# Four-layer transformer on one core: the order of the overlapped pieces of layers three and four rewritten on all five engines

## The chip, the core and the metric

The kernel runs on one NeuronCore of a Trainium2 chip. Its engines are TensorE (PE: matrix products; PEld is its weight load), VectorE (DVE), ScalarE (ACT), GpSimd (POOL) and SyncE (SP, which here only issues DMAs); each runs its own instruction list in order, and they meet by semaphores. The metric is the device time of one execution in microseconds (us).

## The reference

x has 8 sequences (batches) of 512 tokens by 128. Four layers follow one another, each `x = x + attn(layernorm(x)); x = x + ffn(layernorm(x))`. All attentions have 16 heads of 8.

```
layer 1: causal attention without softmax;  ffn = 8 gated experts, two used
layer 2: linear attention with elu+1;       ffn = top-1 of 8 experts (relu), with a capacity
layer 3: softmax attention, |q-k| <= 32;    ffn = silu(x Wg) * (x Wu) Wd, hidden 384
layer 4: rope; k and v from a 64-wide latent; softmax over pages of 32 tokens,
         page(k) <= page(q);                ffn = top-1 of 8 experts (exact gelu, hidden 512)
```

The program counts the layers from 0, so that `l2_` and `l3_` name pieces of layers three and four.

## The kernel before

The program stands in stages with a barrier between them. The table `ORDER2` sets the stage of layers three and four (in the trace from about 481 to 1140 us). For each engine it is a list of pieces; the n-th occurrence of a name is that piece of batch n (0 to 7), here written with the batch behind a dot, `l2_q.4`. A piece is a handful of instructions. The lists are all that decides an engine's order: `for name, b in ORDER2["PE"]` and the like walk through them, and every engine waits by semaphores for what a piece needs. The lists lay layer three of batch b+1 over layer four of batch b. No planner runs inside the kernel; the lists are written out.

The pieces, by what TensorE does in them and the line of its matmuls:

- `l2a_n`, `l2f_n`, `l3a_n`, `l3f_n`: transposes of normalised rows (L611). Ahead of them DVE takes statistics (`..._s`), POOL the power -1/2, DVE normalises; ACT copies the transposes out of PSUM.
- `l2_q` (L899, L900), `l2_v` (L907), `l3_q`, `l3_lat`, `l3_k` (L999), `l3_v` (L1008): projections. `l3_k` comes from the latent that `l3_lat` makes.
- `l2_m0..3` (L917 mask, L925 scores) and `l3_m0..21` (L1022): scores of which DVE takes row maxima (L1701, two reductions a piece; L1710, one a piece). `l2_n1`/`l3_n1` (POOL) and `l2_n2`/`l3_n2` (L672) bring the maxima as extra rows into the stacked Q and K.
- `l2_e0..3` (L939, L948) and `l3_e0..9` (L1039): scores again, less the maximum, transposed; ACT takes exp (L1981, L1993). `l2_o0..3` (L962) and `l3_b0..9` (L1055): products with V. `l3_b` writes to a PSUM bank of its own and takes no buffer of the ring named below.
- `l2_t`, `l2_u`, `l2_j` (L645, L654, L663), and the same for `l3`: transposes, division, output projection; DVE adds it to x (L1162). `l2f_0..2` and `l2f_o` (L976, L977, L985): the feed-forward part of layer three. `l3t_r` (L626), `l3t_c`: router of layer four.

The queries and keys are split into three bf16 parts (`l2_p1`, `l2_p2`, `l3_p1`, `l3_p2` on ACT and POOL) and spread over partitions by 12 DMAs a batch and layer, which SP issues one after the other (L2233), from `l2_p2` or `l3_p2` in its list. `l3_m0` of a batch waits for all 12 of its batch. For batch 0 ACT issues five of them.

PSUM has a ring of three buffers for this stage. Each piece takes one (`l2_m`, `l2_e`, `l3_e`: two) in the order of TensorE's list, and a buffer is free when its reader has drained it. So a piece waits too for the reader of the piece three buffers back.

Of the kernel before, what the change touches and what calls it, by code (L numbers as in the profile page):

```python
# [149 lines left out]
for n in range(4, len(PLAN3)):  # L150
# [40 lines left out]
        l2a_n l2_q l2_v l2_m0 l2_m1 l2a_n l2_m2 l2_m3 l2_n2 l2_q l2_e0 l2_e1 l2_o0 l2_e2 l2_o1 l2_e3 l2_o2 l2_o3 l2_t l2_u l2_j l2_v l2a_n l2f_n  # L191
        l2f_0 l2f_1 l2f_2 l2_q l2f_o l2_m0 l3a_n l3_q l3_lat l3_k l3_v l2_m1 l2_m2 l2_m3 l2_n2 l3_m0 l3_m1 l2_e0 l3_m2 l2_e1 l3_m3 l3_m4 l2_o0 l2_e2
        l3_m5 l3_m6 l2_o1 l2_e3 l3_m7 l2_o2 l3_m8 l3_m9 l3_m10 l2_o3 l2_t l3_m11 l3_m12 l2_u l3_m13 l3_m14 l2_j l3_m15 l3_m16 l3_m17 l2_v l3_m18
        l2f_n l3_m19 l3_m20 l2f_0 l2f_1 l3_m21 l2f_2 l3_n2 l2f_o l3_e0 l2_m0 l3_e1 l3_b0 l2_m1 l3a_n l3_b1 l3_e2 l3_q l3_lat l3_e3 l3_k l3_b2 l3_v
        l2_m2 l3_e4 l3_b3 l2_m3 l3_e5 l3_b4 l3_e6 l3_b5 l2_n2 l2a_n l3_e7 l3_b6 l3_m0 l3_e8 l3_m1 l2_e0 l3_m2 l2_e1 l3_m3 l3_m4 l2_o0 l3_m5 l2_q
        l3_m6 l3_m7 l2_o1 l3_m8 l2_e2 l3_m9 l2_e3 l3_m10 l2_o2 l3_m11 l3_m12 l2_o3 l3_m13 l2_t l3_m14 l3_b7 l2_u l3_m15 l3_m16 l2_j l3_e9 l3_m17
        l3_m18 l3_b8 l2_v l3_b9 l3_m19 l2f_n l3_m20 l3_m21 l2f_0 l2f_1 l2f_2 l3_n2 l3_t l2f_o l3_e0 l3_u l2_m0 l3_e1 l3_b0 l3_j l3a_n l3_e2 l3_lat
        l3_q l2_m1 l3_b1 l3_k l3_e3 l3_b2 l2_m2 l3_e4 l3_b3 l2_m3 l2a_n l3_v l3_e5 l3_b4 l2_n2 l3f_n l3_e6 l3_b5 l3t_r l3_e7 l3_m0 l2_e0 l3_m1 l2_q
        l3_m2 l3_m3 l2_o0 l2_e1 l3_b6 l3_m4 l3_e8 l2_o1 l3_m5 l2_e2 l3_m6 l2_e3 l3_m7 l3_m8 l2_o2 l3_m9 l3_m10 l3_m11 l2_o3 l2_t l3_b7 l3_m12 l2_u
        l3_m13 l3_m14 l2_j l3_e9 l3_m15 l3_m16 l3_b8 l2_v l3_m17 l2f_n l3_m18 l3_m19 l3_m20 l2f_0 l3_m21 l2f_1 l2f_2 l3_b9 l3_t l3_n2 l2f_o l3_u  # L200
        l3_e0 l2_m0 l3_e1 l3_b0 l3t_c l3_j l3a_n l2_m1 l3_lat l3_q l3_e2 l3_b1 l3_k l3_e3 l3_b2 l3_v l2_m2 l3_e4 l3_b3 l2_m3 l3_e5 l3_b4 l3f_n l3_e6
        l3_b5 l2a_n l3t_r l2_n2 l3_e7 l3_m0 l2_q l3_m1 l2_e0 l3_m2 l3_m3 l3_b6 l2_e1 l3_m4 l2_o0 l3_m5 l2_e2 l3_m6 l3_m7 l2_o1 l3_m8 l2_e3 l3_m9
        l3_m10 l2_o2 l3_e8 l3_m11 l3_m12 l2_o3 l3_m13 l2_t l3_m14 l3_b7 l2_u l3_m15 l2_j l3_e9 l3_m16 l3_m17 l3_b8 l2_v l3_m18 l2f_n l3_m19 l3_m20
        l2f_0 l3_m21 l2f_1 l2f_2 l3_b9 l3_n2 l3_t l3t_c l2f_o l3_e0 l3_u l2_m0 l3_b0 l3_e1 l3_j l3a_n l3_e2 l3_q l3_lat l3_b1 l3_k l3_e3 l3_b2 l2_m1
        l3_e4 l3_b3 l3f_n l2_m2 l2_m3 l3_b4 l3_e5 l3t_r l3_v l2a_n l2_n2 l3_e6 l3_m0 l3_b5 l3_e7 l2_q l3_m1 l2_e0 l3_m2 l2_e1 l3_m3 l3_m4 l2_o0 l2_e2
        l3_m5 l3_m6 l2_o1 l3_m7 l3_m8 l2_o2 l3_m9 l2_e3 l3_m10 l3_m11 l3_b6 l3_m12 l2_o3 l3_m13 l2_t l3_e8 l3_m14 l2_u l3_m15 l3_m16 l2_j l2_v l3_m17
        l3_b7 l3_m18 l3_b8 l3_e9 l3_m19 l2f_n l3_m20 l3_m21 l2f_0 l2f_1 l2f_2 l3_n2 l3_b9 l3_t l3t_c l2f_o l3_e0 l3_u l2_m0 l3_e1 l3_b0 l2_m1 l3_j
        l3a_n l3_e2 l3_q l3_lat l3_b1 l3_e3 l3_k l3_b2 l3_v l2_m2 l3_e4 l3_b3 l2a_n l2_m3 l3_e5 l3_b4 l3f_n l3_e6 l3_b5 l2_n2 l3t_r l3_e7 l2_q l3_m0
        l2_e0 l3_m1 l2_e1 l3_m2 l3_b6 l3_m3 l3_e8 l2_o0 l3_m4 l2_e2 l3_m5 l3_m6 l2_o1 l2_e3 l3_m7 l3_m8 l2_o2 l3_m9 l3_m10 l3_m11 l2_o3 l2_t l3_m12
        l3_m13 l2_u l3_m14 l3_b7 l3_m15 l2_j l3_m16 l3_e9 l3_b8 l3_m17 l3_m18 l2_v l3_b9 l3_m19 l2f_n l3_m20 l3_m21 l2f_0 l2f_1 l2f_2 l3_n2 l3_t  # L210
        l2f_o l3_e0 l3_u l2_m0 l3_e1 l3_b0 l3t_c l3_j l3a_n l2_m1 l3_q l3_lat l3_e2 l3_k l3_b1 l3_e3 l3_b2 l2_m2 l3f_n l2_m3 l3t_r l3_e4 l3_b3 l3_e5
        l3_b4 l3_e6 l2_n2 l3_b5 l3_e7 l3_m0 l3_m1 l3_b6 l3_m2 l2_e0 l3_m3 l2_e1 l3_m4 l3_m5 l2_o0 l3_m6 l2_e2 l3_m7 l3_m8 l2_o1 l3_m9 l3_e8 l3_m10
        l2_e3 l3_m11 l3_m12 l2_o2 l3_m13 l3_m14 l2_o3 l2_t l3_v l3_m15 l2_u l3_m16 l3_m17 l2_j l3_b7 l3_e9 l3_m18 l3_m19 l3_b8 l3_b9 l2f_n l3_m20
        l3_m21 l2f_0 l2f_1 l2f_2 l3_t l3_n2 l2f_o l3_u l3t_c l3_e0 l3_e1 l3_b0 l3a_n l3_j l3_q l3_lat l3_k l3_e2 l3_b1 l3f_n l3_e3 l3_b2 l3t_r l3_e4
        l3_b3 l3_e5 l3_b4 l3_e6 l3_b5 l3_m0 l3_m1 l3_m2 l3_m3 l3_b6 l3_v l3_m4 l3_m5 l3_e7 l3_m6 l3_m7 l3_m8 l3_m9 l3_m10 l3_b7 l3_m11 l3_e8 l3_m12
        l3_e9 l3_m13 l3_m14 l3_m15 l3_m16 l3_b8 l3_m17 l3_m18 l3_m19 l3_b9 l3_m20 l3_m21 l3_n2 l3t_c l3_t l3_e0 l3_u l3_e1 l3_b0 l3_j l3_e2 l3_b1
        l3_e3 l3_b2 l3_e4 l3_b3 l3_e5 l3_b4 l3f_n l3_e6 l3_b5 l3t_r l3_e7 l3_b6 l3_e8 l3_b7 l3_e9 l3_b8 l3t_c l3_b9 l3_t l3_u l3_j l3f_n l3t_r l3t_c
    """,
# [2275 lines left out]
```

## Time and profile before

| what | us |
|---|---|
| runs | 1254.84, 1254.14, 1248.28; median 1254.14 |
| the profiled execution, its own time | 1255.06 |
| its span | 1253.3 |
| the stage of layers three and four in it | about 481 to 1140 |
| TensorE busy in the span | 1050.0 |

The span is from the first to the last instruction in the trace; 1.8 us of the profiled execution lie around it. In the view of stretches, each row gives the length of a stretch, what each engine was busy in it, and the clock that TensorE was granted as a share of 2.4 GHz. In the view in order of time, a row is a start, a duration, and in brackets the idle time before it with what ended that.

### The profile page before, as it was taken

Reading aid. Unit: us, or ns where it says so; the run is one execution under the profiler, and the core shown is the slowest. Engines: PE = TensorE matmul, PEld = TensorE weight load, DVE = VectorE, ACT = ScalarE, POOL = GpSimd, SP = SyncE. Lnnn points to the kernel's source line nnn. Section 1 sums busy time; section 2 is a strip of 40 time slices with the busy share of each in tenths; the row PEclk is TensorE's granted clock in tenths of the full one; section 3 lists DMA queues with packets and bytes.
Section 4 is the critical chain, followed back from the end, with each engine's and each line's share of the span. In section 5 each row is a group of like instructions: output and inputs, shape, how many; then the busy total and the mean of one; then the engine's idle time right before and its main releaser. Section 6 shows DMA issues by size and latency. Waiting matters only on the chain.

```text
span 1253.3 us, 38908 instructions
## 1 busy us (share of the span) xinstructions
PE 1050.0 (84%) x16739; PEld 769.8 (61%) x16739; DVE 821.0 (66%) x2329; ACT 553.8 (44%) x993; POOL 448.6 (36%) x538
## 2 busy tenths in 40 slices
PE   6889859999976996776888889888888887987984
PEld 4767637888864573544556656556665555463884
DVE  6889865679965113466769587786958685735332
ACT  4233202476642331333374656556484655261441
POOL 2134341336755244033122315042332404022675
PEclk9899979999976999999999999999999999998998
DMA  9464515643240413114022222112222202002884
GB/s 366 191 236 193 212 41 186 215 157 98 66 163 32 140 52 88 30 53 103 16 64 65 55 54 62 44 48 57 68 60 65 63 3 72 10 23 83 204 191 93
DMA packets 83725, 126.02 MB, mean 101 GB/s; under 512 B 13025, under 2 KB 64610, under 8 KB 83138
## 3 DMA queue, kind: packets, MB, share of 16 engines
q1 hardware_dynamic: 66863, 106.47, 26.5%
q0 software_dynamic: 10928, 13.64, 4.5%
q10 hardware_dynamic: 5763, 3.43, 1.1%
q8 instruction: 131, 2.15, 0.7%
q14 instruction: 40, 0.33, 0.1%
HBM read 50.82 MB, written 46.74 MB: 78 GB/s over the span
## 4 chain that ended last, share of the span: by engine, by line
PE 40%; DVE 26%; POOL 8%; issue 8%; ACT 7%; DMA 7%; SPq 3%; PEldq 1%; ACTq 0%; DVEq 0%; POOLq 0%; PEld 0%
DVE mx L1710 7%; POOL xs L2131 3%; PE ps L1022 2%; SPq L2233 2%; ACT MW L1993 2%; PE ps L787 2%; PE ps L774 2%; PE ps L775 2%; DMA K<-spm 2%; PE ps L962 2%; PE ps L880 2%; PE ps L865 2%; PE ps L976 2%; DVE bst L1134 2%; PE ps L1055 2%
## 5 line engine op out<-in xcount | busy, mean ns | idle before, releaser
L1710 DVE TENSOR_REDUCE mx<-ps 128x2 f32<-128x1024 f32 (+3 forms) x176 | 191.0, 1122 | 52.2 <-PE ps L1022 51.8
L1993 ACT ACTIVATE MW<-ps 128x1024 f32<-128x1024 f32 x160 | 154.6, 1030 | 81.2 <-PE ps L1039 80.9
L2131 POOL DMA_INDIRECT xs<-xr,sidu x96 | 96.7, 1007 | 122.2 <-DVE sidu L1293 87.5
L2074 POOL TENSOR_SCALAR rst<-bmv 128x4 f32<-128x4 f32 x64 | 16.5, 258 | 339.3 <-DVE bmv L1137 338.6
L1055 PE MATMUL ps<-MW,Vp 128*18 128x128 f32 x2560 | 87.4, 278 | 4.4 <-ACT MW L1993 2.3
L1022 PE MATMUL ps<-K,Q 64*128 64x512 bf16 (+3 forms) x512 | 63.5, 310 | 25.3 <-DMA K<-spm 11.9
L1055 PEld LDWEIGHTS ps<-MW,Vp 128*18 128x18 f32 x2560 | 64.2, 99 | 18.5 <-issue 9.0
L2157 POOL DMA_INDIRECT out_dram<-qf,toku x39 | 60.7, 1556 | 35.8 <-DVE toku L1766 27.6
L1981 ACT ACTIVATE MW<-ps 128x1024 f32<-128x1024 f32 x64 | 61.8, 1033 | 14.0 <-PE ps L948 13.8
L1039 PE MATMUL ps<-Q,K 64*128 64x128 bf16 x1280 | 55.2, 220 | 14.1 <-DVE mx L1701 6.8
L1701 DVE TENSOR_REDUCE mx<-ps 128x8 f32<-128x768 f32 x64 | 57.7, 949 | 12.9 <-PE ps L925 12.9
L1799 ACT COPY XT<-ps 128x512 f32<-128x512 f32 x48 | 28.0, 588 | 84.4 <-PE ps L611 83.7
L1147 DVE TENSOR_SCALAR xr<-X,bmv,rst 128x128 f32<-128x128 f32 x128 | 45.1, 415 | 26.0 <-POOL rst L2077 19.0
L611 PE MATMUL ps<-W,xr 128*128 128x128 f32 x192 | 34.0, 305 | 32.5 <-DVE xr L1147 23.8
L2053 ACT ACTIVATE MW<-ps,MW 128x256 f32<-128x256 f32 (+1 forms) x92 | 34.0, 439 | 60.5 <-PE ps L1100 60.4
L2157 POOL DMA_INDIRECT ys<-xp,toku x38 | 38.0, 1000 | 57.9 <-DVE toku L1553 51.3
L1022 PEld LDWEIGHTS ps<-K,Q 64*128 64x128 bf16 x512 | 19.7, 96 | 62.6 <-issue 31.9
L1039 PEld LDWEIGHTS ps<-Q,K 64*128 64x128 bf16 x1280 | 37.7, 95 | 31.8 <-issue 9.1
L1134 DVE BATCH_NORM_STATS2 bst<-X 128x6 f32<-128x128 f32 x256 | 55.3, 278 | 0.8
L2077 POOL TENSOR_TENSOR rst<-rst,npow 128x4 f32<-128x4 f32 x48 | 50.4, 1050 | 4.0
L1162 DVE TENSOR_TENSOR X<-ps,X 128x512 f32<-128x512 f32 x40 | 27.4, 686 | 35.2 <-PE ps L663 13.3
L611 PEld LDWEIGHTS ps<-W,xr 128*128 128x128 f32 x192 | 23.5, 154 | 40.9 <-issue 27.6
(381 smaller groups left out, 2582.1 us busy)
## 6 DMA issues: line engine op xcount, KB each, us to landing
xs<-hb SPq DMA_DIRECT2D x52, 528.0 KB, 8.9
MW<-l_moe_dram SPq DMA_DIRECT2D x19, 768.0 KB, 5.0
MW<-l_moe_dram SPq DMA_DIRECT2D x20, 578.0 KB, 4.8
Q<-spl SPq DMA_DIRECT2D x48, 128.0 KB
Q<-spm SPq DMA_DIRECT2D x48, 128.0 KB
K<-spl SPq DMA_DIRECT2D x43, 128.0 KB
K<-spm SPq DMA_DIRECT2D x43, 128.0 KB
MW<-l_moe_dram SPq DMA_DIRECT2D x16, 256.0 KB, 5.9
```

The costliest lines, as they stand in the source:

```text
L611: m = PE.transpose(p[:, 128 * t:128 * t + 128], xr_of(key)[:, t, 0:128], ident)
L1022: m = PE.matmul(p[:, o:o + nk], Q3[i][64 * k:64 * k + 64, s, 128 * t:nk], K3[i][64 * k:64 * k + 64, s, 0:nk], start=True, stop=True, tile_ ...
L1039: m = PE.matmul(p[:, o:o + 128], K3[i][64 * k:64 * k + 64, 4 * half + s, 128 * kt:128 * kt + 128], Q3[i][64 * k:64 * k + 64, 4 * half + s, ...
L1055: m = PE.matmul(ps[32 * j:32 * j + 18, 7, at:at + 128], v_window(1, 4 * i + kt, 4 * g + j, side), P3[k % 2][:, col(h)[0] + 128 * col(h)[1] ...
L1134: own.end(V.bn_stats(out=bst[:, k, t, :], in_=X[:, 4 * b + t, :]))
L1701: V.tensor_reduce(out=mx[0][:, :, 4 * half:4 * half + 4, t], in_=p.rearrange("p (e n) -> p e n", e=2)[:, :, 0:384].rearrange("p e (s k) -> ...
L1710: V.tensor_reduce(out=mx[1][:, :, s0:s0 + ns, t], in_=p.rearrange("p (e n) -> p e n", e=2)[:, :, 0:ns * nk].rearrange("p e (s k) -> p e s ...
L1981: A.activation(P2[t % 2][:, 1024 * half:1024 * half + 1024], p, ACT.Exp).then_inc(drained[u], 1)
L1993: A.activation(P3[k % 2][:, 1024 * half:1024 * half + 1024], p, ACT.Exp).then_inc(drained[u], 1)
L2077: G.tensor_tensor(out=rst[:, k, 1, :], in0=rst[:, k, 0, :], in1=npow[:, :], op=ALU.pow).then_inc(rstd_on[k], 1)
L2131: G.indirect_dma_start(out=xs[L], out_offset=bass.IndirectOffsetOnAxis(ap=sidu[:, 4 * b + t:4 * b + t + 1], axis=0), in_=src[:, t, :], in_ ...
L2157: G.indirect_dma_start(out=dst, out_offset=at, in_=y[:, v, :], in_offset=None, compute_op=how).then_inc(y_out[k], 16)
```

## The change

Only the strings of `ORDER2` are changed, on all five engines. The pieces are the same, each engine still runs every piece of every batch once, and the durations of instructions, tiles and semaphores are untouched. As the PSUM ring is dealt out in the order of TensorE's list, the buffer of many pieces changes too.

```diff
 ORDER2 = sequences({
     "PE": """
-        l2a_n l2_q l2_v l2_m0 l2_m1 l2a_n l2_m2 l2_m3 l2_n2 l2_q l2_e0 l2_e1 l2_o0 l2_e2 l2_o1 l2_e3 l2_o2 l2_o3 l2_t l2_u l2_j l2_v l2a_n l2f_n
+        l2a_n l2_q l2_v l2a_n l2_m0 l2_m1 l2_m2 l2_m3 l2_n2 l2_q l2_e0 l2_e1 l2_o0 l2_e2 l2_o1 l2_e3 l2_o2 l2_o3 l2_t l2_u l2_j l2a_n l2_v l2f_n
...
     "SP": """
-        l2_get l2_get l2_get l2_p2 l2_get l2_n2 l2_get l2_p2 l3_p2 l2_get l2_n2 l2_p2 l3_n2 l3_p2 l2_get l2_n2 l2_p2 l3_n2 l2_get l3_p2 l2_n2 l2_p2
+        l2_get l2_get l2_get l2_get l2_p2 l2_get l2_n2 l2_p2 l3_p2 l2_n2 l2_p2 l3_n2 l2_get l3_p2 l2_n2 l2_get l2_p2 l3_n2 l3_p2 l2_n2 l2_get l2_p2
```

Three places on TensorE, as the built programs have them.

The first is where `l3_m0` and `l3_m1` of batch 2 (L1022, 128x128) begin; around them stand `l3_e` of batch 1 (L1039), `l2_e0` of batch 3 (L939, L948) and `l2_q` of batch 4 (L899, L900). Before:

```order
L1039 MATMUL ps<-Q3_1,K3_1 128x128 x16
L1022 MATMUL ps<-K3_0,Q3_0 128x128 x8
L939 MATMUL ps<-cb 128x256 x4
L948 MATMUL ps<-Q2,K2 128x64 x16
L939 MATMUL ps<-cb 128x256 x4
L948 MATMUL ps<-Q2,K2 128x64 x16
L1022 MATMUL ps<-K3_0,Q3_0 128x128 x8
L899 MATMUL ps<-XT,W 128x512
L900 MATMUL ps<-XT,W 128x512
```

And of the change:

```order
L1039 MATMUL ps<-Q3_1,K3_1 128x128 x16
L899 MATMUL ps<-XT,W 128x512
L900 MATMUL ps<-XT,W 128x512
L1039 MATMUL ps<-Q3_1,K3_1 128x128 x16
L1055 MATMUL ps<-MW,Vp1 18x128 x16
L672 MATMUL ps<-cb,msp0 96x128 x2
L1039 MATMUL ps<-Q3_1,K3_1 128x128 x16
L1022 MATMUL ps<-K3_0,Q3_0 128x128 x8
L626 MATMUL ps<-W,oT4 128x8 x4
L1022 MATMUL ps<-K3_0,Q3_0 128x128 x8
L939 MATMUL ps<-cb 128x256 x4
```

`l2_q.4` has moved ahead of `l3_m0.2`, and the router piece `l3t_r.0` (L626) behind it.

The second runs from `l2_j.3` (L663) to `l2f_n.3` (L611, xp0); between them stand `l3_m` of batch 2 (L1022), `l3_b` of batch 1 (L1055) and `l2_v.4` (L907). Before:

```order
L663 MATMUL ps<-W,tco 128x128 x4
L1039 MATMUL ps<-Q3_1,K3_1 128x128 x16
L1022 MATMUL ps<-K3_0,Q3_0 128x512 x4
L1055 MATMUL ps<-MW,Vp1 18x128 x16
L907 MATMUL ps<-W,XT 128x128 x8
L1022 MATMUL ps<-K3_0,Q3_0 128x512 x2
L611 MATMUL ps<-W,xp0 128x128 x4
```

And of the change:

```order
L663 MATMUL ps<-W,tco 128x128 x4
L1039 MATMUL ps<-Q3_1,K3_1 128x128 x16
L1022 MATMUL ps<-K3_0,Q3_0 128x512 x2
L1055 MATMUL ps<-MW,Vp1 18x128 x16
L1022 MATMUL ps<-K3_0,Q3_0 128x512 x2
L907 MATMUL ps<-W,XT 128x128 x8
L1022 MATMUL ps<-K3_0,Q3_0 128x512 x2
L1055 MATMUL ps<-MW,Vp1 18x128 x16
L1022 MATMUL ps<-K3_0,Q3_0 128x512 x2
L611 MATMUL ps<-W,xp0 128x128 x4
```

One more `l3_b` and one more `l3_m` stand between the two.

The third is the projection of layer four of batch 5: `l3_lat` (L992), `l3_k` (L999), `l3_v` (L1008), and `l2_m2` of batch 6 (L917, L925). Before:

```order
L992 MATMUL ps<-tc4,W 128x512
L1055 MATMUL ps<-MW,Vp1 18x128 x16
L1039 MATMUL ps<-Q3_0,K3_0 128x128 x16
L999 MATMUL ps<-rt,W 128x128 x8
L1055 MATMUL ps<-MW,Vp1 18x128 x16
L1008 MATMUL ps<-W,rt 128x128 x4
L917 MATMUL ps<-cb 32x384 x8
L925 MATMUL ps<-K2,Q2 32x96 x32
```

And of the change:

```order
L992 MATMUL ps<-tc4,W 128x512
L917 MATMUL ps<-cb 32x384 x8
L925 MATMUL ps<-K2,Q2 32x96 x32
L917 MATMUL ps<-cb 32x384 x8
L925 MATMUL ps<-K2,Q2 32x96 x32
L1008 MATMUL ps<-W,rt 128x128 x4
L1055 MATMUL ps<-MW,Vp1 18x128 x16
L1039 MATMUL ps<-Q3_0,K3_0 128x128 x16
L999 MATMUL ps<-rt,W 128x128 x8
```

`l2_m2.6` and `l3_v.5` now stand ahead of `l3_k.5`.

## Rows read from the trace of the kernel before

**Rows 1.** The page: the span, and busy time by engine.

```profile
span 1253.3 us, 38908 instructions
PE 1050.0 (84%) x16739; PEld 769.8 (61%) x16739; DVE 821.0 (66%) x2329; ACT 553.8 (44%) x993; POOL 448.6 (36%) x538
```

**Rows 2.** Stretches: start:end, length, busy by engine, TensorE's clock, DMA share, GB/s.

```profile
684.60:697.40 12.80, 12.25 (x318) 8.55 (x316) 9.70 (x28) 7.54 (x10) 4.04 (x7) 1.00 0.06 17
697.40:712.50 15.10, 12.03 (x394) 9.46 (x389) 8.39 (x17) 13.44 (x22) 7.90 (x10) 1.00 0.42 110
712.50:757.80 45.30, 40.55 (x732) 25.99 (x733) 36.44 (x63) 21.71 (x38) 6.87 (x10) 0.92 0.17 45
...
786.00:829.70 43.70, 39.42 (x732) 25.32 (x732) 37.01 (x66) 21.20 (x38) 6.86 (x10) 0.96 0.18 47
857.60:901.50 43.90, 39.14 (x782) 26.50 (x780) 37.05 (x64) 24.76 (x42) 6.82 (x10) 0.99 0.19 49
901.50:915.50 14.00, 12.94 (x331) 9.03 (x334) 9.79 (x29) 8.76 (x12) 7.03 (x9) 1.00 0.07 23
931.10:970.60 39.50, 35.17 (x730) 24.55 (x732) 33.28 (x48) 20.30 (x37) 6.85 (x10) 1.00 0.19 52
982.70:1000.10 17.40, 12.25 (x416) 9.48 (x415) 8.16 (x17) 13.29 (x18) 9.70 (x13) 1.00 0.37 99
1000.10:1040.10 40.00, 34.81 (x720) 24.30 (x721) 33.29 (x49) 17.31 (x27) 2.35 (x6) 0.96 0.04 11
```

**Rows 3.** SP in order of time, and the chain's last transfer: start, duration, what.

```profile
700.93 1.89 SPq L2233 DMA_DIRECT2D Q<-spm  x3
...
709.28 0.53 SPq L2233 DMA_DIRECT2D K<-spm  x1
709.28 3.10 DMA K<-spm
```

**Rows 4.** Waits of TensorE, 615.5 to 970.6: us in total, times, longest.

```profile
PE ps L1039 <- DVE mx L1701: 6.8, 8, 1.8
PE ps L611 <- DVE xp L1147: 5.9, 5, 1.7
```

**Rows 5.** TensorE in order of time, 734 to 755.

```profile
735.93 0.40 PE L1039 MATMUL ps<-Q,K 64*128 64x128 bf16 x8
...
737.83 1.07 PE L1055 MATMUL ps<-MW,Vp 128*18 128x128 f32 x32
...
740.81 0.39 PE L1022 MATMUL ps<-K,Q 64*128 64x512 bf16 x2
742.90 0.63 PE L611 MATMUL ps<-W,xp 128*128 128x128 f32 x4 [1.70 <-DVE xp L1147]
...
745.17 1.78 PE L976 MATMUL ps<-XT,W 128*128 128x512 f32 x2 [0.58 <-DVE mx L1710]
...
749.05 1.12 PE L976 MATMUL ps<-XT,W 128*128 128x512 f32 x2
750.01 1.02 PE L977 MATMUL ps<-XT,W 128*128 128x512 f32 x2
```

**Rows 6.** Groups by line, TensorE, 478 to 1150: busy, mean ns, idle before.

```profile
L925 PE MATMUL ps<-K,Q 64*32 64x96 bf16 x2048 | 29.6, 211 | 12.2 <-DMA K<-spl 10.3 <-issue 1.8
...
L626 PE MATMUL ps<-W,oT 128*128 128x8 f32 x64 | 8.8, 264 | 0.7 <-ACT oT L1799 0.7
...
L1008 PE MATMUL ps<-W,rt 64*128 64x128 f32 x64 | 5.8, 300 | 0.9 <-DVE rt L1666 0.8
```

**Rows 7.** The stage's start in order of time: SP, and TensorE's first wait.

```profile
489.89 0.36 SPq L2335 DMA_DIRECT2D xr<-ys  x1
...
494.03 4.05 SPq L2233 DMA_DIRECT2D Q<-spl  x6
...
503.29 0.52 PE L925 MATMUL ps<-K,Q 64*32 64x96 bf16 x32 [8.97 <-DMA K<-spl]
```

**Rows 8.** VectorE's row maxima of the last batch, 1065.7 to 1093.7.

```profile
L1710 DVE TENSOR_REDUCE mx<-ps 128x2 f32<-128x768 f32 (+3 forms) x21 | 22.6, 1121 | 9.1 <-PE ps L1022 9.1
```

More of the change, by code:

```diff
@@ L195 @@
[L195 to L214, printed above, removed]
@@ new lines @@
+        l3_m6 l2_q l3_m7 l3_m8 l3_m9 l2_e2 l3_m10 l2_e3 l3_m11 l3_m12 l2_o2 l3_m13 l3_m14 l2_o3 l2_t l3_m15 l3_b7 l2_u l3_m16 l3_b8 l3_m17 l2_j l3_e9
+        l3_m18 l2_v l3_m19 l3_b9 l2f_n l3_m20 l3_m21 l2f_0 l2f_1 l2f_2 l3_n2 l3_t l2f_o l3_e0 l3_u l2_m0 l3_e1 l3_b0 l2_m1 l3_j l3a_n l3_b1 l3_e2
+        l3_q l3_lat l3_e3 l3_k l3_v l3_b2 l3_e4 l2a_n l2_m2 l3_b3 l2_m3 l3f_n l3_b4 l3_e5 l2_q l3_e6 l3_b5 l2_n2 l3_e7 l3_m0 l3t_r l3_m1 l2_e0 l3_m2
+        l2_e1 l3_m3 l2_o0 l3_m4 l2_e2 l3_b6 l3_e8 l3_m5 l2_o1 l3_m6 l3_m7 l2_e3 l3_m8 l3_m9 l2_o2 l3_m10 l3_m11 l2_o3 l2_t l3_m12 l3_m13 l2_u l3_m14
@@ new lines @@
+        l3_b7 l3_m15 l2_j l3_e9 l3_m16 l3_b8 l3_m17 l2_v l3_m18 l3_b9 l3_m19 l2f_n l3_m20 l3_m21 l2f_0 l2f_1 l2f_2 l3_n2 l3_t l3t_c l2f_o l3_e0 l3_u
+        l2_m0 l3_e1 l3_b0 l3_j l3a_n l2_m1 l3_q l3_lat l3_b1 l3_e2 l3_k l3_e3 l3_v l2_m2 l3_b2 l3_e4 l2_m3 l3_b3 l3_e5 l2a_n l3f_n l3_b4 l3_e6 l2_n2
+        l3t_r l3_m0 l3_m1 l3_b5 l3_e7 l3_m2 l2_q l3_m3 l2_e0 l3_m4 l2_e1 l3_m5 l2_o0 l3_m6 l2_e2 l3_m7 l2_o1 l2_e3 l3_m8 l2_o2 l3_m9 l3_m10 l3_m11
+        l3_b6 l2_o3 l3_m12 l2_t l3_e8 l3_m13 l2_u l3_m14 l2_j l3_m15 l2_v l3_m16 l3_b7 l3_e9 l3_m17 l3_m18 l3_b8 l2f_n l3_m19 l3_m20 l3_m21 l3_b9
@@ new lines @@
+        l2f_0 l2f_1 l2f_2 l3_n2 l3_t l3t_c l2f_o l3_e0 l3_u l2_m0 l3_b0 l3_e1 l3_j l3a_n l3_e2 l3_q l3_lat l3_b1 l3_k l3_e3 l3_b2 l3_v l2_m1 l2a_n
+        l3f_n l2_m2 l3t_r l2_m3 l3_b3 l3_e4 l2_q l2_n2 l3_e5 l3_m0 l3_b4 l3_m1 l3_m2 l2_e0 l3_m3 l3_e6 l2_o0 l3_m4 l2_e1 l3_m5 l3_m6 l3_b5 l2_e2
+        l3_m7 l3_m8 l2_o1 l3_m9 l2_e3 l3_m10 l3_m11 l2_o2 l3_m12 l3_b6 l3_e7 l3_m13 l2_o3 l3_m14 l2_t l3_e8 l3_m15 l2_u l3_m16 l3_b7 l3_m17 l2_j
+        l3_e9 l3_b8 l3_m18 l2_v l3_m19 l3_b9 l2f_n l3_m20 l3_m21 l2f_0 l2f_1 l2f_2 l3_n2 l3_t l3t_c l2f_o l3_e0 l3_u l2_m0 l3_e1 l3_b0 l2_m1 l3_j
@@ new lines @@
+        l3a_n l3_e2 l3_q l3_lat l2_m2 l3_v l3_b1 l3_e3 l3_k l3_b2 l3_e4 l3_b3 l2_m3 l3_e5 l3_b4 l3f_n l2a_n l3_e6 l3_b5 l2_n2 l3t_r l3_e7 l2_q l3_m0
+        l3_m1 l3_b6 l2_e0 l3_m2 l3_b7 l3_m3 l3_e8 l2_o0 l3_m4 l2_e1 l3_m5 l2_e2 l3_m6 l3_m7 l2_o1 l2_e3 l3_m8 l2_o2 l3_m9 l3_m10 l3_m11 l2_o3 l2_t
+        l3_m12 l2_u l3_m13 l3_m14 l2_j l3_e9 l3_b8 l3_m15 l3_m16 l2_v l3_m17 l2f_n l3_m18 l3_m19 l3_b9 l3_m20 l2f_0 l3_m21 l2f_1 l2f_2 l3_n2 l3_t
+        l3t_c l2f_o l3_e0 l3_u l2_m0 l3_b0 l3_e1 l3_j l3a_n l3_e2 l3_q l3_lat l2_m1 l3_k l3_b1 l3_e3 l3_b2 l2_m2 l3f_n l2_m3 l3_e4 l3_b3 l3t_r l2_n2
```

88 lines of the change are left out of this document (46 added, 42 removed).

## The prediction

> **What bounds the kernel now.** I read the page first. TensorE is busy 1050.0 of 1253.3 us, 84% [rows 1], so an order can win at most what TensorE waits inside the stage, and what low clock stretches there. Next I read that stage in stretches [rows 2]. Each batch of layer four gives three of them, which behave differently; the rows show batch 2 in full.
>
> A is from the end of `l2f_o.2` to the end of `l3_k.2`, 684.6 to 697.4: 12.8 us, TensorE busy 12.25. Layer norm and projections run one after another, and `l3_e`, `l3_b` of the batch before fill the gaps. A is full.
>
> B is from there to the start of `l3_m0.2`: 15.1 us, TensorE busy only 12.03 [rows 2]. B is no matter of TensorE's work. The bf16 parts go out in 12 DMAs; SP begins at 700.93, issues three in 1.89 us (0.63 each), issues the last at 709.28, and that one is the chain's last transfer, 3.10 us [rows 3]. Begin 3.5 us after `l3_k`, 8.4 us of issuing, 3.1 of landing make the 15. Other work in B is free as long as it is under 15 us. `l3_m0` stands in TensorE's list, so all behind it waits too.
>
> C is from `l3_m0.2` to the end of `l2f_o.3`: 45.3 us, TensorE 40.55, VectorE 36.44 [rows 2]. The C of batches 3, 4, 5, 6 are 43.7, 43.9, 39.5 and 40.0 with TensorE 39.42, 39.14, 35.17, 34.81. The difference of length and busy time is 4.75, 4.3, 4.8, 4.3 and 5.2: almost constant, while the lengths differ by 6. So C costs what TensorE has to do in it, plus some 4.7 us of small waits, and of busy time some is low clock: in batch 2's C it was 0.92 on average, in batch 5's 1.00 [rows 2].
>
> So an order gains by moving TensorE's work from C or A into B, by fewer small waits in C, and by fewer falls of the clock in A and C.
>
> **The change part by part.** Prices first. `l3_b` is 32 matmul records, 1.07 us; `l3_e` two times eight, 0.40 each, overlapped to 0.6; an `l3_m` of the late kind 0.39, `l2_q` like the pair 1.12 + 1.02 less overlap, 1.9 [rows 5]. A router piece is 8.8/8 = 1.1; `l3_v` 5.8/8 = 0.7; `l2_m` has 64 of the 2048 records of L925, 29.6/32 = 0.9, and its masks lie mostly under them, 1.0 [rows 6].
>
> Stage start: SP now issues a fourth `l2_get` ahead of the first stack of DMAs. The third begins at 489.89 and takes 0.36 [rows 7]; the fourth needs its landing and a DVE sum, about 493.5 by the 2.7 us that the first get took to its sum, so the stack's first `Q<-spl`, at 494.03 before, starts late by some 1.5 us. Its six took 4.05 us because they also waited for the later parts [rows 7], which swallows most of it. I take +0.6, bounds 0 and +1.5. The second `l2a_n` moves in front of `l2_m0`, into TensorE's wait of 8.97 us [rows 7]: VectorE's eight maxima, not TensorE, set the next step, so no gain.
>
> Batch 1: in its C one more `l3_b` is gone from between `l2_j.2` and `l2f_n.2`, and one maximum fewer stands there on VectorE: +0.3. Batch 2, A: `l3_e3` now ahead of `l3_k`, +0.5.
>
> Batch 2, C, the largest term. First place in the diff: `l2_q.4` leaves C for B (-1.9), `l3t_r.0` enters (+1.1), `l3t_c.0` too (+0.2): -0.6. Second place: one more `l3_b` (1.07) and `l3_m` (0.39) stand ahead of `l2f_n.3`, which waited 1.70 us for VectorE [rows 5]: -1.4. The clock had fallen behind that wait: L976 took 1.78 us there, 1.12 two pieces later [rows 5], and its partner L977 as much longer. If the wait goes, these 1.4 us go. Sum -3.4.
>
> The Trainium skill ("TensorE: Matmul & The Clock Gate", section on HAM oscillation) says that a wait before each burst sends the array back to its low clock, and that the cure is work without the wait; that agrees with these rows in kind. By it the longer wait that I expect ahead of `l3_m0.3` would be paid for as well, which the third rival below prices from rows.
>
> Batch 3, C: `l3_b5` and `l3_e7` of batch 2 come over from B, +1.7; again one `l3_b` and one `l3_m` more ahead of `l2f_n.4`, -1.3 (its own wait was of the same group, 5.9 us in five such waits [rows 4]): +0.4. Batch 4, C: `l2_q.6` out, `l3_b4` and `l3_e6` in, -0.2; one maximum fewer on VectorE ahead of `l2f_n.5`, -0.6. Batch 5, A: third place. `l2_m2.6` (1.0) and `l3_v.5` (0.7) now stand before `l3_k.5`. They were in B, free; now they delay the 15 us chain. A was full (12.94 of 14.0 [rows 2]): +1.6, bounds +0.7 (if 1 us of its idle time absorbs them) and +1.7. Batch 5, C: +0.4, a shorter cover of `l2f_n.6`. Batch 6, C: `l3_e7` in, +0.6, `l3t_c.4` +0.2, one maximum more before `l2f_n.7`, +1.0: +1.8.
>
> The waits of `l3_e4` for the maxima of `l2_m2`, 6.8 us in eight [rows 4], mostly go, since an `l3_b`, which needs no ring buffer, now stands between the two in four batches. They lie in B, and B ends with the twelfth DMA: nothing. If B were TensorE's own, they would be worth up to 5 us.
>
> On POOL, `l2_n1` now stands before `l3_p2` in batches 0, 1 and 5. SP needs the lowest part only for its last two issues, some 7 us after its first [rows 3]; `l2_n1`'s four small operations fit in that. Nothing, while VectorE has finished `l2_m3` by then; else up to +1 each.
>
> Last batch: VectorE waits 9.1 us for TensorE in its 21 maxima [rows 8], 0.4 each as a floor (21 x 0.4 = 8.4) and the rest where an `l3_v` or `l3_e` pair stood between. `l3_e7` leaves it: I take -1.0, bounds -2 and 0. What follows is one dependent chain with its pieces in the same order: nothing.
>
> Sum: 0.6 + 0.3 + 0.5 - 3.4 + 0.4 - 0.8 + 1.6 + 0.4 + 1.8 - 1.0 = +0.4 us, on the profiled execution's 1255.06. That stands 0.9 above the median of the runs, 1254.14. So a median of about 1254.5; I say 1254.
>
> **The rivals.** First (mine): the new order trades equal amounts, 1254. What can be told from no change on this kernel I set at 0.5%, 6.3 us. Chance 0.43.
>
> Second: the interleave inside C is better throughout. The 4.7 us of small waits in a C times seven batches with a full overlap are 33 us, and my sum touches only those ahead of `l2f_n`. If each C loses 1.8 of its 4.7 us, 12.6 us go: 1254.5 - 12.6 = 1242. For it: the maxima on VectorE need 36.44 us in a C of 45.3 [rows 2], so it isn't at its limit. Against: TensorE's ring has three buffers, and the pieces' readers are what they were. Above 0.9 us per C it becomes a measurable gain. Chance of a gain past 0.5%: 0.32.
>
> Third, on the other side: the clock. Less of TensorE's work lies in B (batch 3 -1.7, batch 5 -1.7, batch 6 -0.6, and the shorter `l3_e4`, about 1 us in four batches), so it waits longer ahead of `l3_m0`: 15 less 12.03 was 3.1 us of idle time in B, now 4 to 6. Then the clock is low when C begins, where TensorE's time counts. A fall costs 1.4 us or a bit more [rows 5]. Two such Cs had a mean clock of 0.92 and 0.96 and two 0.99 or 1.00 [rows 2]. Falls in all seven instead of three, 4 x 1.7 = 7 us, on top of +0.4: 1262. It decides if four more Cs show a mean clock under 0.97. Chance of a loss past 0.5%, by this or by maxima that come too late for SP: 0.25.
>
> **How the numbers follow.** Forecast 1254. The bounds of the unknown terms (start 0 to +1.5, batch 5 -0.9 to 0, last batch -1 to +1) make 1252 to 1257 for my case alone; with partial gains or losses in C it is 1248 to 1260. Eight in ten must reach to both others: 1243 to 1263. Faster 0.32, same 0.43, slower 0.25.
>
> **What the profile of the changed kernel would show.** B of every batch still 15 to 16 us, whatever TensorE does in it (if batches 2 or 3 fall to 14 or rise over 17, my view of B is wrong). C of batch 2 about 42, C of batch 3 about 44, A of batch 5 near 15.5. The wait ahead of `l2f_n.3` under 0.5 us and no clock fall behind it. The group of `l3_e4` waits (L1039 for L1701) from 6.8 to under 3 us, without a gain in B. Differences of length and busy time in C of 4 to 5.5 us. The prediction is wrong if those differences change by 1 us or more in most batches, or if the mean clock in the Cs does.

## The result, and the profile after

The changed kernel takes 1262.29 us (median of 20 runs, 1255.26 to 1268.7); the kernel before took 1255.97 beside it (20 runs). The ratio is 1.0053, 95% interval 1.0036 to 1.0071: 6.7 us slower. I had said 1254, no change.

The page of the changed kernel, first lines, to be held against [rows 1]. The profiled execution itself took 1259.9 us.

```profile
span 1258.1 us, 38909 instructions
PE 1059.5 (84%) x16739; PEld 776.4 (62%) x16739; DVE 824.3 (66%) x2329; ACT 552.5 (44%) x993; POOL 447.9 (36%) x538
```

TensorE issues the same 16739 matmuls and is busy 9.5 us longer. That is low clock: the mean granted clock of this execution is 0.941 against 0.951, and busy time times clock agrees within 0.2%. One execution holds some luck. The stretches, cut at the same pieces as in [rows 2]: B of batch 0, then B2, C2, B3, C3, A5, B5, C5, B6, C6.

```profile
559.40:572.40 13.00, 8.40 (x180) 4.61 (x182) 5.04 (x7) 3.04 (x8) 6.79 (x9) 0.87 0.56 126
...
696.20:712.00 15.80, 12.59 (x377) 8.67 (x376) 8.58 (x23) 12.86 (x22) 9.31 (x13) 1.00 0.40 104
712.00:753.10 41.10, 37.44 (x738) 26.41 (x740) 35.85 (x67) 20.75 (x37) 6.84 (x10) 0.96 0.21 57
...
765.60:784.40 18.80, 13.54 (x348) 10.17 (x346) 11.10 (x19) 12.69 (x20) 10.44 (x14) 0.82 0.34 91
784.40:828.20 43.80, 38.84 (x785) 26.59 (x786) 36.32 (x66) 22.84 (x40) 6.87 (x10) 1.00 0.19 49
...
900.50:916.30 15.80, 14.57 (x418) 10.27 (x418) 11.53 (x30) 9.50 (x16) 7.10 (x9) 1.00 0.06 20
916.30:931.50 15.20, 11.80 (x296) 8.49 (x298) 6.44 (x15) 13.20 (x19) 7.59 (x10) 1.00 0.41 108
931.50:975.10 43.60, 38.21 (x728) 25.59 (x728) 35.59 (x57) 19.58 (x35) 6.86 (x10) 0.92 0.18 47
...
987.40:1003.00 15.60, 11.50 (x400) 8.99 (x402) 9.13 (x18) 10.68 (x14) 7.81 (x10) 1.00 0.41 108
1003.00:1044.10 41.10, 35.59 (x738) 24.46 (x739) 34.60 (x57) 19.30 (x30) 2.35 (x6) 0.96 0.04 11
```

Two stretches stand out: B of batch 3 is 18.8 us at a clock of 0.82, and C of batch 5 is 43.6 at 0.92, where [rows 2] has 39.5 at 1.00. C2 is 41.1, where about 42 was forecast. The waits of TensorE from 612.5 to 975.1, to be held against [rows 4]:

```profile
PE ps L1022 <- DMA K<-spm: 8.2, 4, 3.0
PE ps L611 <- DVE xp L1147: 3.3, 2, 2.0
...
PE ps L1039 <- DVE mx L1701: 0.5, 1, 0.5
```

The waits of `l3_e4` are gone (6.8 to 0.5). Those ahead of `l2f_n` fell from 5.9 in five to 3.3 in two. The waits of `l3_m0` for the last stack of DMAs add up to 8.2 in four. In the kernel before that line read:

```profile
PE ps L1022 <- DMA K<-spm: 4.1, 4, 1.4
```

### Why VectorE was late for `l2f_n`

TensorE and VectorE in batch 5 of the changed kernel, with the GpSimd rows between them, in order of time:

```profile
956.77 1.15 POOL L2096 TENSOR_TENSOR qf<-qf,spl 128x512 f32<-128x512 f32 x1
...
957.53 2.10 DVE L1147 TENSOR_SCALAR xp<-X,bmv,rst 128x128 f32<-128x128 f32 x4
...
957.88 1.15 POOL L2096 TENSOR_TENSOR kf<-kf,spl 128x512 f32<-128x512 f32 x1
...
959.78 1.04 PE L611 MATMUL ps<-W,xp 128*128 128x128 f32 x4 [2.04 <-DVE xp L1147]
...
961.71 1.80 PE L1055 MATMUL ps<-MW,Vp 128*18 128x128 f32 x32
```

The same place in the kernel before:

```profile
945.30 1.16 POOL L2096 TENSOR_TENSOR qf<-qf,spl 128x512 f32<-128x512 f32 x1 [18.69 <-ACT spl L1818]
...
957.46 1.11 DVE L1147 TENSOR_SCALAR xp<-X,bmv,rst 128x128 f32<-128x128 f32 x4
...
958.71 0.63 PE L611 MATMUL ps<-W,xp 128*128 128x128 f32 x4 [0.41 <-DVE xp L1147]
```

The four operations of `l2f_n.6` take 1.11 us alone and 2.10 while GpSimd does the subtractions of `l2_p1.7`. The new order moved `l2_p1.7` directly behind `l2f_s.6` on GpSimd, and `l2f_n.6` runs just then. TensorE waits 2.04 instead of 0.41, and behind that wait it is at its low level (granted clock 0.53 from 959.6 to 963.2): `l3_b` takes 1.80, at full clock 1.07 [rows 5]. So the durations of instructions, which I had called untouched by the change, are not. In the kernel before the same collision lay over `l2f_n.2`, `.3`, `.4`, `.5` (2.1 us each); in the changed one over `.1` (1.95), `.5` (2.81) and `.6`.

The one at `l2f_n.1`, in C0, is new too: the old order had `l2_p2.2` ahead of `l2f_s.1` on GpSimd, the new one has it behind. How hard it hits differs from execution to execution. In the changed kernel's profile GpSimd starts 0.6 us behind VectorE:

```profile
597.88 1.95 DVE L1147 TENSOR_SCALAR xp<-X,bmv,rst 128x128 f32<-128x128 f32 x4
599.88 0.66 PE L611 MATMUL ps<-W,xp 128*128 128x128 f32 x4 [0.83 <-DVE xp L1147]
```

In that of `after_five`, which has the same pieces there, it starts 0.2 us behind:

```profile
594.97 2.80 DVE L1147 TENSOR_SCALAR xp<-X,bmv,rst 128x128 f32<-128x128 f32 x4
595.15 1.18 POOL L2103 TENSOR_TENSOR spl<-qf,spl 128x512 bf16<-128x512 f32 x1 [0.89 <-ACT spl L1833]
597.83 1.11 PE L611 MATMUL ps<-W,xp 128*128 128x128 f32 x4 [2.15 <-DVE xp L1147]
```

Seven of the eleven profiles of the new order have the long form, with a C0 of 43.1 us on average, and four the short one, with 40.3.

The Trainium skill ("SBUF — State Buffer", section on who interferes with whom) says that VectorE and GpSimd share a port pair as an exclusive lock, taken by a `tensor_scalar` in its two-port form or by an operation with two inputs in SBUF. The trace agrees: with 1.5 us of GpSimd's two operations left when L1147 starts it takes 1.0 us longer, with 2.2 left 1.7 longer, and L1710, which reads PSUM, takes 1.22 us with or without them.

### Stretches of all profiles together

A stretch whose pieces an experiment doesn't touch is one more sample of its order. Length in us from the views in order of time, mean (lowest to highest, number of profiles), and what the prediction had for the difference:

| stretch | old order | new order | difference | predicted |
|---|---|---|---|---|
| start, to the end of `l2f_o.0` | 62.5 (7) | 63.4 (9) | +0.9 | +0.6 |
| A0 + B0 + C0 | 65.3 (3 to 5) | 66.0 (9 to 11) | +0.7 | 0 |
| A1 + B1 + C1 | 69.7 (3 to 5) | 69.7 (10, 11) | 0.0 | +0.3 |
| A2 | 12.8 (12.8 to 12.8, 5) | 13.4 (13.4 to 13.4, 11) | +0.6 | +0.5 |
| B2 | 15.0 (14.7 to 15.1, 4) | 15.8 (15.5 to 16.4, 11) | +0.9 | 0 |
| C2 | 44.7 (44.1 to 45.3, 2) | 41.9 (41.2 to 42.5, 10) | -2.9 | -3.4 |
| B3 | 16.4 (15.6 to 16.9, 6) | 18.5 (17.2 to 19.1, 4) | +2.1 | 0 |
| A3 + C3 | 56.1 (5) | 56.7 (8, 9) | +0.6 | +0.4 |
| A4 + B4 + C4 | 73.6 (5 to 7) | 72.9 (6 to 9) | -0.7 | -0.8 |
| A5 | 14.0 (13.9 to 14.4, 8) | 15.8 (15.8 to 15.8, 5) | +1.8 | +1.6 |
| B5 | 15.4 (15.0 to 15.8, 8) | 15.3 (14.9 to 15.7, 5) | -0.1 | 0 |
| C5 | 39.5 (39.5 to 39.7, 8) | 42.4 (41.4 to 43.7, 5) | +2.9 | +0.4 |
| B6 | 17.4 (17.1 to 17.8, 7) | 16.0 (15.6 to 16.6, 8) | -1.5 | 0 |
| A6 + C6 | 52.0 (8) | 53.7 (8) | +1.7 | +1.8 |
| last batch and end | 101.1 (8) | 102.3 (8) | +1.3 | -1.0 |

The differences are those of the unrounded means. They add up to +8.0; the runs say +6.7. Most of it is batch 5 (+4.5) and batch 3 (+2.6). Behind the small sum of batch 0 stand two large terms: B0 is 1.5 us shorter (14.7 to 13.2) and C0 2.2 longer (39.9 to 42.1).

### The profile page after: what moved, and what is told of

The parts are those of the page before. It is cut to its first block, busy times and chain, and to the rows that moved or that the text cites. A ratio compares the mean times of both kernels' runs of the same rounds, so it can differ in the third digit from the quotient of the medians.

```text
span 1258.1 us, 38909 instructions
## 1 busy us (share of the span) xinstructions
PE 1059.5 (84%) x16739; PEld 776.4 (62%) x16739; DVE 824.3 (66%) x2329; ACT 552.5 (44%) x993; POOL 447.9 (36%) x538
## 4 chain that ended last, share of the span: by engine, by line
PE 46%; DVE 21%; ACT 9%; DMA 7%; issue 6%; POOL 5%; SPq 4%; PEldq 1%; DVEq 0%; ACTq 0%; PEld 0%; POOLq 0%
DVE mx L1710 5%; ACT MW L1993 4%; PE ps L1055 3%; SPq L2233 3%; PE ps L1022 2%; PE ps L880 2%; PE ps L962 2%; PE ps L787 2%; PE ps L865 2%; PE ps L774 2%; PE ps L775 2%; PE ps L976 2%; POOL xs L2131 2%; DVE bst L1134 2%; PE ps L985 2%
## 5 line engine op out<-in xcount | busy, mean ns | idle before, releaser
L1710 DVE TENSOR_REDUCE mx<-ps 128x2 f32<-128x1024 f32 (+3 forms) x176 | 191.3, 1123 | 57.0 <-PE ps L1022 56.0
L2074 POOL TENSOR_SCALAR rst<-bmv 128x4 f32<-128x4 f32 x64 | 16.4, 256 | 294.5 <-DVE bmv L1137 293.8
L1055 PE MATMUL ps<-MW,Vp 128*18 128x128 f32 x2560 | 89.2, 282 | 2.5 <-ACT MW L1993 1.8
L1022 PE MATMUL ps<-K,Q 64*128 64x512 bf16 (+3 forms) x512 | 65.1, 317 | 27.5 <-DMA K<-spm 14.2
L1055 PEld LDWEIGHTS ps<-MW,Vp 128*18 128x18 f32 x2560 | 65.4, 100 | 18.2 <-issue 10.2
L1701 DVE TENSOR_REDUCE mx<-ps 128x8 f32<-128x768 f32 x64 | 58.0, 952 | 14.0 <-PE ps L925 12.9
L1039 PE MATMUL ps<-Q,K 64*128 64x128 bf16 x1280 | 54.6, 220 | 12.3 <-ACT MW L1993 7.7
L611 PE MATMUL ps<-W,xr 128*128 128x128 f32 x192 | 34.4, 310 | 33.7 <-DVE xr L1147 25.8
L1022 PEld LDWEIGHTS ps<-K,Q 64*128 64x128 bf16 x512 | 20.0, 97 | 59.3 <-issue 27.5
L1039 PEld LDWEIGHTS ps<-Q,K 64*128 64x128 bf16 x1280 | 37.2, 95 | 31.4 <-ACT MW L1993 11.3
L1147 DVE TENSOR_SCALAR xr<-X,bmv,rst 128x128 f32<-128x128 f32 x128 | 45.4, 418 | 13.7 <-POOL rst L2077 9.2
L611 PEld LDWEIGHTS ps<-W,xr 128*128 128x128 f32 x192 | 23.9, 156 | 41.9 <-issue 21.2
```

The lines of the kernel that those rows point to most:

```text
L611: m = PE.transpose(p[:, 128 * t:128 * t + 128], xr_of(key)[:, t, 0:128], ident)
L1022: m = PE.matmul(p[:, o:o + nk], Q3[i][64 * k:64 * k + 64, s, 128 * t:nk], K3[i][64 * k:64 * k + 64, s, 0:nk], start=True, stop=True, tile_ ...
L1039: m = PE.matmul(p[:, o:o + 128], K3[i][64 * k:64 * k + 64, 4 * half + s, 128 * kt:128 * kt + 128], Q3[i][64 * k:64 * k + 64, 4 * half + s, ...
L1055: m = PE.matmul(ps[32 * j:32 * j + 18, 7, at:at + 128], v_window(1, 4 * i + kt, 4 * g + j, side), P3[k % 2][:, col(h)[0] + 128 * col(h)[1] ...
L1701: V.tensor_reduce(out=mx[0][:, :, 4 * half:4 * half + 4, t], in_=p.rearrange("p (e n) -> p e n", e=2)[:, :, 0:384].rearrange("p e (s k) -> ...
L1710: V.tensor_reduce(out=mx[1][:, :, s0:s0 + ns, t], in_=p.rearrange("p (e n) -> p e n", e=2)[:, :, 0:ns * nk].rearrange("p e (s k) -> p e s ...
```

## The experiments

Times are medians, ratios are to the kernel before on the same chip, with the 95% interval, and the clock is the mean over the kernel's runs. Beside them the kernel before had medians of 1253.8 to 1255.8 and a mean clock of 0.947; the changed kernel 0.941.

| kernel | us | ratio | clock |
|---|---|---|---|
| head_before | 1267.92 | 1.0107 (1.0074 to 1.014) | 0.939 |
| to3_after | 1258.27 | 1.0022 (0.9995 to 1.0049) | 0.943 |
| mid_after | 1260.05 | 1.0047 (1.002 to 1.0073) | 0.942 |
| to5_after | 1257.39 | 1.0028 (1.0005 to 1.0052) | 0.942 |
| after_three | 1260.24 | 1.005 (1.0024 to 1.0075) | 0.940 |
| before_pool | 1249.47 | 0.9957 (0.993 to 0.9983) | 0.949 |
| after_hit | 1269.84 | 1.0124 (1.0088 to 1.0159) | 0.940 |
| before_q4 | 1254.73 | 0.9996 (0.9972 to 1.002) | 0.945 |
| best | 1247.94 | 0.9972 (0.9946 to 0.9997) | 0.948 |
| after_b3_norm | 1262.66 | 1.0088 (1.0054 to 1.0123) | 0.941 |
| after_b3_add | 1265.45 | 1.0098 (1.0064 to 1.0132) | 0.941 |
| after_four | 1256.49 | 1.0023 (0.9998 to 1.0049) | 0.946 |
| before_add7 | 1255.98 | 1.0008 (0.9985 to 1.0032) | 0.947 |
| after_five | 1257.15 | 1.0019 (0.9994 to 1.0043) | 0.942 |

### Half old, half new

Each engine's list is one order up to a piece, and the other order's rest behind it (`old[:p]` is what had begun when TensorE ended piece p):

```diff
-ORDER2 = new
+ORDER2 = old[:l2f_o.0] + rest of new                              # head_before
+ORDER2 = new[:l2f_o.3] + rest of old                              # to3_after
+ORDER2 = old[:l2f_o.0] + rest of new[:l2f_o.3] + rest of old      # mid_after
+ORDER2 = new[:l2f_o.5] + rest of old                              # to5_after
```

head_before. 

> The new order, but with the old one on all engines up to the end of l2f_o.0. By the two profiled executions the new stage start costs +3.8 us (17.8 + 46.1 against 15.6 + 44.5 us). If the loss sits in single places (theory 1), this kernel is 6.7 - 3.8 = 2.9 us slower than the kernel before. If the loss is spread over the whole stage as small waits and falls of the clock (theory 2), the start holds only its share of the stage's length, 62 of 656 us, and it is about 6 us slower.

to3_after. 

> The new order up to the end of l2f_o.3 on all engines, the old one from there. By the stretches of the two profiled executions: start +3.8, batch 0 -2.6, batch 1 +1.1, batch 2 -2.8, so -0.5 us against the kernel before (theory 1). If the loss is spread evenly (theory 2), 268 of the stage's 656 us are new, so +2.7 us.

mid_after. 

> The old order up to l2f_o.0, the new one from there to the end of l2f_o.3, the old one behind it. Theory 1: the new order's good part alone, -2.6 + 1.1 - 2.8 = -4.3 us against the kernel before, faster than both. Theory 2 (spread loss): +2 us.

to5_after. 

> The new order up to the end of l2f_o.5, the old one from there. By the stretches: -0.5 for what lies before, batch 3 +3.2, batch 4 +0.5, so +3.2 us against the kernel before (theory 1); what is left to the whole loss of 6.7 is batch 5. Theory 2: 415 of 656 us are new, +4.2 us; the two theories are told apart by the step from the order that is new up to l2f_o.3 to this one: +3.7 us in 147 us of stage against +1.5.

As totals they told little. Where the old start is joined to the new rest, A0 is 17.7 us instead of 10.7 (in both kernels that have this seam), so head_before and mid_after carry 7 us of their own: mid_after's +0.47% says nothing against the gain in batch 2. The step from to3_after to to5_after was to be 3.7 us by theory 1 and came out at +0.06% with an uncertainty of some 0.35%: it decides nothing. What they gave is repeats of stretches: A5 15.8 again in head_before, C5 41.4 there and 39.5 or 39.6 in the other three, B3 18.8 and 19.1. The new order's stretches are long in the same places each time (B3 17.2 to 19.1 in four profiles, C5 41.4 to 43.7 in five). So the loss has places (theory 1); the 3.8 us that I had given the start were mostly luck of one execution (+0.9 over sixteen).

### The moves on VectorE, GpSimd and SyncE

before_pool keeps every piece of TensorE and ScalarE where the kernel before has it:

```diff
     "POOL": """
...
-  l3_p2 l2_n1 l2f_s l2_p1 l3_n1          (l2f_s.2; the same swap at l2f_s.4 and l2f_s.5)
+  l3_p2 l2_n1 l2_p1 l2f_s l3_n1
...
-  l2_p1 l2f_s l2_p2 l3_n1                (l2f_s.3)
+  l2_p1 l2f_s l3_n1 l2_p2
...
     "SP": """
-  l2_p2 l3_p2 l2_get l2_n2 l2_p2 l3_n2 l3_p2
+  l2_p2 l3_p2 l2_n2 l2_p2 l3_n2 l2_get l3_p2
```

> The old order with five moves on GpSimd and SyncE alone: l2_p1.3, l2_p1.5, l2_p1.6 ahead of l2f_s.2, l2f_s.4, l2f_s.5, l2_p2.4 behind l3_n1.2 (so that VectorE's l2f_n.2 to l2f_n.5 run free), and l2_get.5 behind l3_n2.0 (so that its load does not share the queues with the last parts of l3_p2.0). Theory A: l2f_n.2, .3, .4, .5 fall from 2.1 to 1.1 us each; C1, C2, C3, C4 each 1 us shorter, 2.7 where a fall of the clock goes too; B0 from 15.2 to 13.1. In all -6 us, faster than both kernels. Theory B (VectorE is not late for TensorE in C): the four normalisations are shorter and the Cs stay as they were, B0 unchanged, 0 us.

It is faster than both: 0.9957. In its profile `l2f_n.2` to `.5` take 1.1 us each, and TensorE's waits ahead of them are 0, 0.69, 0.25 and 0.72 instead of 0.79, 1.70, 1.27 and 1.73: 1.0 less at each, where there was that much. C1 to C4 are 0.4, 2.7, 1.0 and 0.3 us shorter than in the profile of before. Over both profiles that have these moves (the other is that of best) they are 41.1, 41.9, 42.5 and 43.0 on average, and over the two to five of the old order without them 41.7, 44.7, 43.4 and 45.2. A3 pays 0.8 of it back: 13.5 in both, 12.6 or 12.7 without. Its C2, where the clock is 0.96 on average instead of 0.92 [rows 2]:

```profile
715.70:758.40 42.70, 39.11 (x732) 25.49 (x733) 35.48 (x64) 22.16 (x39) 6.89 (x10) 0.96 0.18 47
```

B0 fell from 15.2 to 13.8 (14.2 to 15.2 in three profiles with the load `l2_get.5` in its old place, 13.7 and 13.8 in two without it). In the chain of the kernel before, SyncE starts that load just ahead of the last stack, which ScalarE issues here, and the stack's transfer takes 5.33 us:

```profile
569.14 0.59 SPq L2335 DMA_DIRECT2D xr<-ys  x1
...
569.38 5.33 DMA K<-spm
```

In before_pool, which issues that load at 617.0, the same stack takes 3.86. In the changed kernel, which issues it at 611.4, SyncE issues the last stack, and it takes 3.53.

after_hit puts the collision into the new order, at `l2f_s.2`, `.3` and `.4`:

```diff
     "POOL": """
-  l3_p2 l2_p1 l2f_s l3_n1 l2_p2          (l2f_s.2; the same swap at l2f_s.3 and l2f_s.4)
+  l3_p2 l2f_s l2_p1 l3_n1 l2_p2
```

> The new order with the collision added in three batches: on GpSimd l2_p1.3, l2_p1.4, l2_p1.5 directly behind l2f_s.2, l2f_s.3, l2f_s.4, so over VectorE's l2f_n.2, .3, .4, which took 1.1 us each. Theory A: these take 2.1 each, and C1, C2, C3 are 1 us longer each, up to 2.7 with a fall of the clock behind the wait: +3 to +8 us on the new kernel, so +10 to +15 on the one before. Theory B: 0 us on the new kernel.

`l2f_n.2`, `.3` and `.4` took 2.81, 2.13 and 2.12 us. The ratio went from 1.0053 to 1.0124, 8.9 us where theory A allowed up to 8, but the stretches of its profile explain less: TensorE's waits ahead of the three are 1.65, 0.36 and 0, since in batches 3 and 4 the `l3_b` and `l3_m` that the new order has put ahead of `l2f_n` cover VectorE's lateness. C1 was 1.0 us longer, C2 and C3 0.3 each. The rest of the 8.9 us (uncertain by some 5) has no place in its one profile.

after_three, after_four and after_five mend the new order step by step:

```diff
     "DVE": """
-  l3_q l3f_s l2_add l3_k l2_m2 l2_m3 l3f_n         (batch 3, with l2_add.7, l3f_n.1)
+  l2_add l3_q l3f_s l3_k l3f_n l2_m2 l2_m3
     "POOL": """
-  l2f_s l2_p1                                      (l2f_s.5 and l2f_s.6)
+  l2_p1 l2f_s
     "ACT": """
-  l2_o2 l2_o3 l3t_w l2_u l3_e9 l2_p1               (l2_p1.7)
+  l2_o2 l2_p1 l2_o3 l3t_w l2_u l3_e9
     "PE": """
-  l3_lat l2_m2 l3_v l3_b1 l3_e3 l3_k l3_b2         (l3_k.5; VectorE and ScalarE alike)
+  l3_lat l3_b1 l3_e3 l3_k l3_b2 l3_v l2_m2
     "ACT": """                                       (after_four and after_five)
-  l3_e4 l3_p1 l3_e5                                (l3_p1.5)
+  l3_p1 l3_e4 l3_e5
     "ACT" and "POOL":                              (after_five alone)
-  l3_e5 l3f_n l3_p2                                (ScalarE, l3_p2.5)
+  l3_p2 l3_e5 l3f_n
-  l3_p1 l2_n1 l3_p2                                (GpSimd, l3_p2.5)
+  l3_p1 l3_p2 l2_n1
```

after_three. 

> The new order with three places mended, each in a stretch of its own. B of batch 3: VectorE does l3f_n.1 ahead of l2_m2.4 again and l2_add.7 ahead of l3_q.3. C of batches 4 and 5: GpSimd does l2_p1.6 ahead of l2f_s.5 and l2_p1.7 ahead of l2f_s.6 (ScalarE's l2_p1.7 earlier too), so that no GpSimd tensor operation lies over VectorE's l2f_n.5 and l2f_n.6, which took 2.81 and 2.10 us under it and 1.1 elsewhere. A of batch 5: l2_m2.6 and l3_v.5 behind l3_k.5 again. Theory A (order of VectorE and GpSimd, collisions of the two): B3 from 18.8 to 16.2, C4 -1.5, C5 from 43.7 to 41, A5 from 15.8 to 14.1 with B5 still 15 to 15.6, in all about -7.8 us, 1 us under the kernel before. Theory B (the loss is TensorE's own work moved into these stretches, or the clock whatever the engines around it do): only A5 moves, -1.7, and the kernel stays 5 us slower than before.

after_four. 

> The new order with all places mended: the moves of the kernel with three places, and ScalarE's l3_p1.5 ahead of l3_e4.4 as in the old order (behind it SyncE's stacks began 2.5 us later, and B5 was 18.1 us). B3 16.2, C4 44, A5 13.9, B5 15 to 15.5, C5 about 39.5 to 41. Against the new order -8 us of stretches, of which the clock decides how much is seen: a ratio of 0.999 to the kernel before. If the third rival of the prediction is right, the wait ahead of l3_m0.5 (2.2 us in the new order, 0.5 in the old) has let the clock fall at the start of C5, and with l2_m2.6 and l3_v.5 back in B5 it does not fall there.

after_five. 

> The new order with four places mended, and in B of batch 5 now also ScalarE's l3_p2.5 ahead of l3_e5.4 and GpSimd's l3_p2.5 ahead of l2_n1.6, as in the old order. With l3_p1.5 alone in its place, the first six stacks began 3.5 us after l3_k.5, but the last six only from 922.4 on, since ScalarE's l3_p2.5 stood behind l3f_n.3 and GpSimd's behind l2_n1.6, and B5 was 17.5. If B is the chain over five engines up to the twelfth stack, B5 falls to 15 to 15.6, and the kernel is 1.5 to 2 us faster than with four. If TensorE's own pieces in B5 (l2_m2.6, l3_v.5 back in it) are the bound, B5 stays at 17.5.

In the three profiles B3 is 16.2, 16.8 and 15.8, C4 43.8, 42.8 and 42.8, A5 13.9 and C5 40.4, 40.5 and 40.6; the waits ahead of `l2f_n.5` and `.6` are 0 and 1.05 instead of 1.27 and 2.04. B5 is what I had not foreseen: 18.1, 17.5, then 15.2. SyncE's stacks of batch 5 in after_four:

```profile
915.43 1.91 SPq L2233 DMA_DIRECT2D Q<-spm  x3
917.38 1.92 SPq L2233 DMA_DIRECT2D K<-spm  x3
922.38 1.17 SPq L2233 DMA_DIRECT2D Q<-spm  x2
...
926.89 0.60 SPq L2233 DMA_DIRECT2D K<-spm  x1
```

And in after_five, where ScalarE's and GpSimd's `l3_p2.5` stand ahead of what they had waited behind:

```profile
915.17 1.93 SPq L2233 DMA_DIRECT2D Q<-spm  x3
917.14 1.89 SPq L2233 DMA_DIRECT2D K<-spm  x3
919.08 2.35 SPq L2233 DMA_DIRECT2D Q<-spm  x2
...
923.41 1.38 SPq L2233 DMA_DIRECT2D K<-spm  x1
```

The pause of 3 us after the sixth stack is gone, with TensorE's pieces untouched. So B is the chain `l3_k`, VectorE, GpSimd, ScalarE's and GpSimd's `l3_p1` and `l3_p2`, SyncE; a piece that waits ahead of any of them on any of these engines lengthens it. As a whole the mended stretches of after_five are 8.7 us shorter than the new order's means, and the ratio fell from 1.0053 to 1.0019, 4.3 us, uncertain by some 4. I can't say whether the missing half is chance. None of the three kernels mends `l2f_n.1`: in the profiles of after_three and after_five it has its long form, and C0 is 44.4 and 44.9, longer than in all others.

after_b3_norm and after_b3_add do the two VectorE moves of batch 3 one at a time, before_add7 the second one in the other direction:

```diff
     "DVE": """
-  l3_k l2_m2 l2_m3 l3f_n                           (new order, after_b3_norm)
+  l3_k l3f_n l2_m2 l2_m3
-  l3_q l3f_s l2_add l3_k                           (new order, after_b3_add)
+  l2_add l3_q l3f_s l3_k
-  l2_add l3_q l3f_s l3_k                           (old order, before_add7)
+  l3_q l3f_s l2_add l3_k
```

after_b3_norm. 

> The new order with one move: VectorE's l3f_n.1 ahead of l2_m2.4, as in the old one. B of batch 3 was 18.8, 18.8, 19.1 and 17.2 us in four profiles of the new order and 16.2 with this move and that of l2_add.7. If TensorE's list is the bound (l3t_r.1, ahead of l3_m0.3, waits for l3f_n.1), this move alone brings B3 to about 17, where the stacks end. If the stacks are the bound (l2_add.7 delays l3_k.3's rope on VectorE), B3 stays 18.8.

after_b3_add. 

> The new order with one move: VectorE's l2_add.7 ahead of l3_q.3, as in the old one. If TensorE's list is the bound, SyncE's stacks begin 2 us sooner after l3_k.3, and B3 stays at 18 to 19 us. If the stacks are the bound, B3 falls to about 17.

before_add7. 

> The old order with one move: VectorE's l2_add.7 between l3f_s.1 and l3_k.3, as in the new one, instead of ahead of l3_q.3. In the new order this place cost B of batch 3 some 2.5 us (18.5 with it; 16.3 and 16.2 without it). If VectorE's queue ahead of l3_k.3 is the cause, B3 of the old order goes from 15.6 to 16.9 up to about 18.5, and l2_add.7 takes 2.8 us under GpSimd's operations instead of 1.1. If the cause was another part of the new order, B3 stays under 17.

B3 was 17.6, 16.3 and 16.4. The last stack is issued 14.1 us after `l3_k.3` in the changed kernel, 13.7 with `l3f_n.1` moved, 12.6 with `l2_add.7` moved (12.9 in the kernel before). So `l2_add.7` is the larger cause, and not the only one. How TensorE's list takes part, in the changed kernel:

```profile
764.81 2.82 DVE L1687 SCALAR_TENSOR_TENSOR X<-xr,gate,X 128x128 f32<-128x128 f32 x4
...
768.88 0.58 PE L1008 MATMUL ps<-W,rt 64*128 64x128 f32 x2 [1.99 <-DVE rt L1666]
...
778.85 1.02 PE L611 MATMUL ps<-W,xr 128*128 128x128 f32 x4 [1.81 <-DVE xr L1147]
...
779.68 0.60 SPq L2233 DMA_DIRECT2D K<-spm  x1
779.79 1.91 PE L1055 MATMUL ps<-MW,Vp 128*18 128x128 f32 x32
...
783.42 1.06 PE L626 MATMUL ps<-W,oT 128*128 128x8 f32 x8 [0.60 <-ACT MW L1993]
...
784.41 0.62 PE L1022 MATMUL ps<-K,Q 64*128 64x128 bf16 x16
```

`l2_add.7` (2.82 us under GpSimd's operations, 1.17 in after_b3_add) delays `l3_k.3` on VectorE, so `l3_v.3` waits 1.99; `l3f_n.1` waits 1.81; behind each wait the clock is low (`l3_b` 1.91); and `l3_m0.3` starts directly behind `l3t_r.1`, with no wait for a stack. This B was TensorE's own. In the old order before_add7's `l2_add.7` took 1.98, the stacks began 0.8 us later, and the last one still left after 12.9: there the delay found room. Its total (1.0008) shows nothing either. The totals of the two one-move kernels, six runs each, lie above the changed kernel's, where the stretches would put them below; within their intervals they can't be told from it.

### `l2_q.4` alone, and the best version

```diff
     "PE": """
-  l3f_n l3_e6 l3_b5 l3t_r l3_e7 l3_m0 l2_e0 l3_m1 l2_q     (old order, l2_q.4; ScalarE alike)
+  l3f_n l2_q l3_e6 l3_b5 l3t_r l3_e7 l3_m0 l2_e0 l3_m1
```

> The old order with one piece moved: l2_q.4 ahead of l3_e6.1 on TensorE and ScalarE, from the C of batch 2 into its B. My term in the prediction was -1.9 us for C2 at no cost in B2, whose length SyncE's stacks set: C2 from 45.3 to 43.4, B2 still 15 to 16. If B is TensorE's own there (12.03 of 15.1 us busy, so 14 of 15 after the move), B2 grows by up to 1.9 and nothing is won.

B2 became 16.1, C2 44.7: together 60.8 where the profile of before has 60.5 and that of before_add7 59.3. Even C2 by itself isn't clearly shorter (45.3 and 44.1 in those two). The chain that ends B2 in before_q4:

```profile
709.83 0.29 ACT qf L1947
...
710.32 0.58 ACT kf L1948
710.90 1.84 ACT MW L1993 x2
712.75 0.27 ACT tmpA L2007
713.01 1.85 ACT MW L1993 x2
```

The last stack was issued at 708.85, 11.9 us after `l3_k.2` as in [rows 3]; `l3_m0.2` started at 713.04 straight behind `l3_e7.1`. ScalarE's copies of `l2_q.4` stand ahead of the exponentials, and TensorE's `l3_e7` waits for ScalarE's buffers. So B was TensorE's and ScalarE's own once 1.9 us were put into it: nothing is won.

best is before_pool with two more moves:

```diff
     "POOL": """
-  l3_k l3_p1 l2_n1 l3_p2                           (old order, l3_p2.6, l2_n1.7)
+  l3_k l3_p1 l3_p2 l2_n1
     "SP": """
-  l3_p2 l2_get l2_n2                               (l2_get.6)
+  l3_p2 l2_n2 l2_get
```

> The old order with the five moves that made it 0.43% faster, and two more: on GpSimd l3_p2.6 ahead of l2_n1.7, on SyncE l2_get.6 behind l2_n2.2. The B of batch 6 is 17.1 to 17.8 us in every profile of the old order, since GpSimd's l3_p2.6 stands behind l2_n1.7, which waits for the maxima of l2_m3.7; with it ahead, B6 is about 15.5. The load l2_get.6 no longer starts beside the last stacks of l3_p2.1: B1 from 15.8 to 15 at best. Together -2 to -3 us on top of -5.4, so about -0.6% against the kernel before. If l2_n1 ahead of l3_p2 costs nothing, as the prediction had it, B6 stays 17.4 and the ratio stays 0.996.

Its median, 1247.94, is the lowest of all, but the kernel before was faster beside it too, and its ratio is 0.9972 (0.9946 to 0.9997), where before_pool's is 0.9957. So it is faster than both kernels by little more than its uncertainty, and not measurably different from before_pool. The two moves did what the prediction said of such moves, next to nothing: B6 17.1, B1 15.8. In B6 the last stack now leaves 13.0 us after `l3_k.6` instead of 13.7, but lands after 4.1 instead of 3.7.

## Why the prediction was wrong

Two steps of it failed. "Other work in B is free as long as it is under 15 us" set every change of a B to nothing; the Bs changed by +2.1 (B3), +0.9 (B2) and -1.5 (B0, B6). And the terms of the Cs took VectorE's time for `l2f_n` as given, where GpSimd's order sets it at 1.1 to 2.8 us; that is a part of the +2.9 in C5, forecast as +0.4, and of the +2.2 in C0, forecast as nothing.

**Start** (+0.6, bounds 0 to 1.5): +0.9 over sixteen profiles, inside the bounds. **A2, A5, batch 4 as a whole, A and C of batches 3 and 6**: each within 0.2 us of its term. A5 is the clearest: two pieces ahead of `l3_k.5` cost +1.8, as a full A must.

**C2** (-3.4): the size is right (-2.9), the working only in part, so some of it is luck. `l2f_n.3`'s wait went from 1.70 to 0. One more `l3_b` and `l3_m` do that almost alone (with the collision put back, in after_hit, the wait is 0.36 and C2 42.2), and taking the collision away does as much for C2 (before_pool and best, with the old pieces, have a wait of 0.69 and 42.7 and 41.2). The changed kernel has both, and only the first was in the sum. The term of `l2_q.4` and the router pieces, -0.6, is too small to be seen beside that.

**B2** (0, measured +0.9) is the first place of the step on B. In the changed kernel TensorE isn't what lengthens it: in all eleven profiles of the new order TensorE still waits ahead of `l3_m0.2`, 0.7 to 1.9 us. The first stack leaves later, 4.3 us after `l3_k.2` instead of 3.5. In all eleven ScalarE is at the exponentials of an `l3_e` when GpSimd has `l3_p1.2`'s input ready, and in the five of the old order it is idle then:

```profile
697.69 1.27 POOL L2194 TENSOR_TENSOR rr<-rr,rt 128x512 f32<-128x512 f32 x1 [0.22 <-DVE rt L1666]
698.02 1.94 ACT L1993 ACTIVATE MW<-ps 128x1024 f32<-128x1024 f32 x2
699.84 1.14 ACT L1818 CAST spm<-rr 128x512 bf16<-128x512 f32 x2
```

TensorE's own work can bound a B too: with `l2_q.4` put into the old B2 alone, in before_q4, the wait ahead of `l3_m0.2` is gone and nothing is won. The room there was not 15.1 less 12.03 but that wait, 1.2 us; the rest of the idle time lay at `l3_e4` (1.5), where the moved work did not use it.

**B3** (0, measured +2.1): same step, and I had named the sign of it: B3 over 17. I read the chain of B from SyncE's start only. What stands ahead of `l3_k` and `l3_p1`, `l3_p2` on VectorE, ScalarE and GpSimd decides when SyncE can start; I had looked at GpSimd for `l2_n1` alone. **B6 and B0** are the same miss with the other sign: -1.5 in B6, where the first stack leaves 3.9 us after `l3_k.6` instead of 5.0, and -1.5 in B0, of which one load moved gives 0.9 to 1.4.

**C5** (+0.4, measured +2.9) is the largest single miss. I counted TensorE's cover ahead of `l2f_n.6` and took VectorE's time for it as given. It is 1.1 or 2.1 us, by what GpSimd does at that moment, and the view in order of time had it: four of the old order's `l2f_n` at 2.1, each beside a row of GpSimd, and the others at 1.1. The profiles divide the 2.9. With the clock at 1.00 throughout, the new C5 is 41.4 (two profiles), +1.9; with `l2_p1.7` moved away as well it is 40.5, so the collision is 0.9, if the pieces of A5 and B5 that the same kernels moved back cost C5 nothing. The remaining 1.0 lies in the order of the pieces in C5 and stays undivided. Where the clock fell it was 42.6, 43.0 and 43.7, on the mean of five profiles +1.0.

**C0** (nothing, measured +2.2): the collision at `l2f_n.1` shown above. No experiment takes it away, so the sizes 43.1 and 40.3 are a comparison of profiles, not a test.

**The last batch** (-1.0, measured +1.3) fell outside its bounds, and no experiment bears on it. Its profiles fall into two groups. In four of the eight of the new order TensorE is at its low level for 13.7 to 17.1 us around B7, and the batch is about 3 us longer; in the other four it is as long as in the old order. Of the old order's eight, one is as long, with 10.2 us at the low level. Why TensorE is held there is not shown. B7 in after_five, where the changed kernel has 15.5 us at a clock of 0.89:

```profile
1049.10:1066.40 17.30, 14.09 (x254) 10.71 (x252) 3.43 (x12) 11.08 (x15) 6.04 (x6) 0.67 0.35 93
```

Of the other signs that I had named, length less busy time in C moved by 1 us or more in two of five (C2 4.8 to 3.7, C5 4.3 to 5.4), so not in most.

**The rivals.** The second (C better throughout) is refuted as a whole. The third, the clock, gave the right time, 1262, and its mechanism is there in part. TensorE's wait for the last stack doubled (4.1 to 8.2), as it said. The first 12 us of C5, in the new order of head_before, where `l3_m0.5` had waited 1.96 us:

```profile
939.20:951.20 12.00, 11.02 (x392) 8.58 (x394) 9.28 (x11) 8.24 (x11) 0.00 (x0) 1.00 0.03 7
```

And in after_b3_norm, with the same pieces there, where it had waited 2.49:

```profile
935.60:947.60 12.00, 11.28 (x332) 8.22 (x336) 8.26 (x10) 7.68 (x9) 0.00 (x0) 0.86 0.03 6
```

In the three profiles of the new C5 with a wait of 2.2 to 2.8 us ahead of `l3_m0.5` the clock is low at its start, in the two with 1.0 and 2.0 it isn't, and in the eight of the old order (0 to 0.8) and the three mended ones (0.2 to 1.6) it never is. The fall costs 1.2 to 1.6 us of C5 (42.6 and 43.0 against 41.4), near the 1.7 that I had priced. Pieces taken out of B5 therefore cost twice, once in A5 and in some executions once more through the clock in C5. At other places the wait alone doesn't sort the profiles: after 2.7 us ahead of `l3_m0.6` (after_four) the clock stayed high, and after 1.56 (before_pool) it fell. My condition, four more Cs under 0.97, failed: six against four, where the prediction had counted three. The falls in B3 sit behind waits inside B.

Over whole runs the mean clock fell from 0.947 to 0.941. Among runs of one kernel a clock lower by 0.001 goes with 0.65 us (one slope fitted to all kernels), so 0.006 would be 4 of the 6.7 us if the same slope holds between the two kernels, which isn't shown. For C5 sixteen profiles without an exception tie the fall to the wait; elsewhere it is argued from their order in time.

## What to carry to other kernels

When pieces move, read each moved piece against what the *other* engines do at that moment: a two-input or `tensor_scalar` operation of VectorE under GpSimd tensor operations took 1.7 to 2.5 times its time here, and five moves on GpSimd and SyncE, neither of them the bound, made the kernel 0.4% faster where rewriting all five lists made it slower. The room for extra work in a stretch that ends with a transfer is the wait directly ahead of the instruction that needs it, not the stretch's idle time; and the transfer itself leaves late when a piece of any engine stands ahead of what feeds it. And a stretch that nobody touched is a free repeat: here an A repeats to 0.5 us, most Bs to 1.4, most Cs to 2, while the runs of one kernel lie some 12 us apart.

## What the hardware showed that I had not expected

- L1147 on VectorE, four operations on 128x128: 1.11 us alone, 2.10 when it started with 0.4 us left of the first of two GpSimd operations of 1.15 us, 2.81 when it started just behind the start of the first.
- The last 128 KB stack of batch 0 landed 3.86 us after its issue with no load beside it (before_pool), 5.33 and 5.09 with one `l2_get` started 0.24 us ahead of it (before, before_add7), and 4.32 with one started 0.29 us behind it (before_q4).
- After a wait of 2.2 to 2.8 us TensorE was granted its low level (1.2 GHz) at the start of C5, and after 2.0 it was not; ahead of `l3_m0.6` there was a wait of 2.7 us without a fall and one of 1.56 with a fall.
- The time of a run of one kernel goes with its mean clock, some 0.65 us for each 0.001, over a spread of some 12 us.
